# Attention, layer norm and a mixture of experts on one core: two early projections, one transfer for the row maxima, and the norm stage's tail mixed with the first shared block

## The reference

```python
q = q * cos + rotate_half(q) * sin;  k = k * cos + rotate_half(k) * sin
attn = softmax(einsum('bqhd,bkhd->bhqk', q, k) * scale);  out = einsum('bhqk,bkhd->bqhd', attn, v)
x = layernorm(x + out @ Wo)
normed = x * rsqrt(mean(x ** 2) + 1e-08) * norm_weight
shared = relu(normed @ sw1 + sb1) @ sw2 + sb2
probs = sigmoid(normed @ router_w.T);  scores, idx = top_k(probs, 2)
w = scores / (sum(scores) + 1e-06)
routed = sum over the two chosen e of w_e * (relu(normed @ ew1[e] + eb1[e]) @ ew2[e] + eb2[e])
x = layernorm(x + shared + routed)
```

## Time and profile before

| | |
|---|---|
| median of 3 runs | 1240.48 us (1239.56 to 1247.5) |
| the profiled execution's own time | 1242.63 us |
| its span in the trace | 1240.8 us |
| mean granted TensorE clock | 0.975 of full speed |
| busy: PE, PEld, DVE, ACT, POOL | 1168.7, 860.3, 940.9, 897.4, 580.9 us |

### The profile page before, as it was taken

How to read it: one execution, slowest core, us unless ns; L and a number is a source line. 1 busy time by engine, 2 the same in 40 slices (tenths; PEclk the granted TensorE clock), 3 DMA queues, 4 the chain that set the end, 5 groups by cost and what they waited for, 6 DMA issues and landing times. The chain is left out here.

```text
span 1240.8 us, 25922 instructions
## 1 busy us (share of the span) xinstructions
PE 1168.7 (94%) x8416; PEld 860.3 (69%) x8416; DVE 940.9 (76%) x1865; ACT 897.4 (72%) x1979; POOL 580.9 (47%) x593
## 2 busy tenths in 40 slices
PE   4799999999999999899999799999999999999897
PEld 3233333333333332278999799999999999999897
DVE  5788888888888888288666568777777777777596
ACT  5388878887788776667545367777777777777686
POOL 6232323232232200046567646666666666666763
PEclk9699999999999999999899989999999999999999
DMA  6854645565554620151132277767777777776363
GB/s 150 150 111 101 150 112 138 113 144 119 125 117 106 133 70 19 35 179 35 57 112 92 93 223 257 256 232 230 260 248 235 236 258 244 233 243 208 131 207 110
DMA packets 260826, 194.50 MB, mean 157 GB/s; under 512 B 152272, under 2 KB 243664, under 8 KB 260752
## 3 DMA queue, kind: packets, MB, share of 16 engines
q1 hardware_dynamic: 253936, 174.82, 49.8%
q0 software_dynamic: 6816, 18.75, 4.2%
HBM read 122.06 MB, written 37.52 MB: 129 GB/s over the span
## 5 line engine op out<-in xcount | busy, mean ns | idle before, releaser
L561 DVE TENSOR_REDUCE att_mx<-att_psA 128x1 f32<-128x512 f32 x512 | 328.0, 680 | 83.8 <-PE att_psA L359 83.5
L469 ACT ACTIVATE att_prob<-att_psB 128x512 f32<-128x512 f32 x512 | 293.6, 606 | 102.7 <-PE att_psB L371 100.9
L359 PE MATMUL att_psA<-att_qk 96*128 96x512 bf16 x512 | 199.0, 392 | 16.3 <-DMA att_qk<-att_prob 8.7
L371 PE MATMUL att_psB<-att_qk 128*128 128x512 bf16 x512 | 195.5, 385 | 7.7 <-DMA att_qk<-att_mrow 6.8
L1650 ACT ACTIVATE exp_psU<-exp_psU,ew_b 128x256 f32<-128x256 f32 x312 | 126.7, 447 | 103.6 <-PE exp_psU L1607 103.6
L1701 DVE CAST exp_hh<-exp_psU 128x512 fp32r<-128x512 f32 x156 | 107.8, 691 | 102.1 <-ACT exp_psU L1650 102.1
L1590 PE MATMUL exp_psD<-exp_w2h,exp_hh 128*128 128x256 f32 x624 | 175.8, 282 | 0.0
L1605 PE MATMUL exp_psU<-exp_xh,exp_w1h 128*128 128x256 f32 x624 | 173.8, 278 | 1.4 <-DVE exp_xl L1692 1.4
L1607 PE MATMUL exp_psU<-exp_xh,exp_w1l 128*128 128x256 f32 x624 | 173.3, 278 | 0.0
L1606 PE MATMUL exp_psU<-exp_xl,exp_w1h 128*128 128x256 f32 x624 | 173.3, 278 | 0.0
L1591 PE MATMUL exp_psD<-exp_w2l,exp_hh 128*128 128x256 f32 x624 | 172.4, 276 | 0.0
(11 more groups left out here) (236 smaller groups left out, 2779.7 us busy)
## 6 DMA issues: line engine op xcount, KB each, us to landing
ew_w<-ew SPq DMA_DIRECT2D x40, 1024.0 KB, 5.6
exp_w<-ew SPq DMA_DIRECT2D x38, 1024.0 KB, 5.8
slots_x<-pre_acc SPq DMA_DIRECT2D x13, 780.0 KB, 4.4
pre_spare<-slots_x SPq DMA_DIRECT2D x39, 260.0 KB, 4.2
out_g<-rows_y SPq DMA_DIRECT2D x32, 256.0 KB, 4.0
ew_b<-eb SPq DMA_DIRECT2D x39, 128.0 KB
pre_spare<-xT SPq DMA_DIRECT2D x8, 512.0 KB, 5.1
attn_rows<-att_ob SPq DMA_DIRECT2D x8, 512.0 KB, 2.8
```

The costliest lines, as they stand in the source:

```text
L359: pe.matmul(psA[A_BANK[n % U]][:, :], r[:, 0, qt * P:(qt + 1) * P], r[:, 1, :], start=True, stop=True).then_inc(s_amm, 1)
L371: pe.matmul(psB[B_BANK[n % U]][:, :], r[:, 1, kt * P:(kt + 1) * P], r[:, 0, :], start=True, stop=True).then_inc(s_bmm, 1)
L469: act.activation(prob[:, n % PR, :], psB[B_BANK[n % U]][:, :], ACT.Exp, scale=SCALE).then_inc(s_exp, 1)
L561: dve.reduce_max(mx[:, g % 2, n % U:n % U + 1], psA[A_BANK[n % U]][:, :], AX_X).then_inc(s_max, 1)
```

## The change

Three things are changed.

- **Early projections.** The query and key projections of tiles 5 and 6 are made right behind that of tile 4, ahead of the first row blocks of scores, into the free banks psB[0] and psB[1]; their rotations go to period -2 and to the end of period -1. `score_cols(1)` waits for the second.
- **Maxima.** `place_max` moves the three pieces with one transfer (48 partitions to 3) in place of three (16 partitions to 1 each).
- **Norm tail and dispatch.** PE's and ACT's slots from 34 on move into the shared stage. From slot 36 on, four slots begin with one chunk of `up` of block 0. Ahead of slot 35, ACT makes `rows_hi` of block 0 and the sigmoid of tiles 0 to 23. DVE makes `rows_lo` of block 0 and chooses the experts of those 24 tiles ahead of the wait for the norm stage, and those of the last 8 behind it. PE counts the ranks ahead of chunk 7 of block 0 instead of behind it. The eight scans become one. POOL does `hidden_lo` for block 0 only; DVE does it for block 1, behind `place`, and `rows_lo` of block 1 also goes behind `place`. POOL's memset goes to the front.

```diff
+    LATE_ASIDE, EARLY_QK = (2, 3), (5, 6)
+    EARLY_ROPE = ((FILL, ROPE[-1]), (FILL + 1, U - 1))
...
             def place_max(g):
                 sp.wait_ge(s_mev, g + 1)
-                for k in range(PIECES):
-                    sp.dma_start(qk[96 + k:97 + k, g // HG % 2, 0, heads(g), :].rearrange("o j (t c) -> o (j t) c", c=P),
-                                 mrow[k * U:(k + 1) * U, g % 2, :]).then_inc(s_mld[g % 2], 16)
+                sp.dma_start(qk[KR:KR + PIECES, g // HG % 2, 0, heads(g), :].rearrange("o j (t c) -> o (j t) c", c=P),
+                             mrow[:, g % 2, :]).then_inc(s_mld[g % 2], 16)
...
+                if n == 1:
+                    pe.wait_ge(s_qrd, EARLY_QK[1] + 1)
...
+                        if p + QK_LEAD == FILL:
+                            for tile in EARLY_QK:
+                                project(tile, False)
...
+    AHEAD, POOLED = 2, 1
+    CHOSEN = TILES - 2 * QT
+    UP_FROM, UP_IN_TAIL, RANK_BEFORE = tail.first + 2, 4, 7
...
+            for slot in range(tail.first, tail.end):
+                if slot == UP_FROM:
+                    for s, v in (tail.turned, tail.residual, tail.split):
+                        pe.wait_ge(s, v)
+                if 0 <= slot - UP_FROM < UP_IN_TAIL:
+                    shared.up(pe, Nth(0), slot - UP_FROM, slot - UP_FROM + 1)
+                tail.tensor(pe, slot)
...
+            for slot in range(tail.first, tail.end):
+                if slot == UP_FROM - 1:
+                    act.wait_ge(*tail.transposed)
+                    shared.rows_hi(act, Nth(0))
+                    act.wait_ge(*tail.residual)
+                    probabilities(slice(0, CHOSEN))
+                tail.scalar(act, slot)
             pr.after_last(act)
+            probabilities(slice(CHOSEN, TILES))
...
+            dve.wait_ge(s_k, 32)
+            shared.rows_lo(dve, Nth(0))
+            link(choose(0, slice(0, CHOSEN)))
             pr.after_last(dve)
-            shared.rows_lo(dve, Nth(0))
-            choose()
-            shared.rows_lo(dve, Nth(1))
+            link(dve.memset(ones[:, :], 1.0))
+            choose(1, slice(CHOSEN, TILES)).then_inc(s_both, 1)
+            weigh()
             place()
-            shared.rows_lo(dve, Nth(2))
+            for n in range(POOLED, AHEAD):
+                shared.rows_lo(dve, Nth(n))
+                Nth(n).wait(dve, shared.lo_ready, shared.HC, 0)
+                for h in range(shared.HC):
+                    shared.hidden_lo(dve, Nth(n), h)
+            shared.rows_lo(dve, Nth(AHEAD))
```

267 lines of the change are left out of this document (142 added, 125 removed).

## The result

| | before | changed |
|---|---|---|
| median of 20 runs each | 1243.08 us (1238.6 to 1247.5) | 1236.99 us (1232.12 to 1241.31) |
| ratio | | 0.9946, 95% interval 0.9933 to 0.9959 |
| own time of the profiled execution | 1242.63 us | 1234.07 us |
| its span | 1240.8 us | 1232.2 us |
| start of the norm stage (PE's first turning) | 523.59 | 514.83 |

The change makes the kernel 6.7 us faster by the ratio (5.1 to 8.3 by its interval), and the two medians are 6.1 us apart. The forecast was 12.7 us; 1236.99 us lies above the range. The two profiled executions are 8.6 us apart: 8.8 us had been won when the norm stage began, and from there to the load of tile 0 the changed kernel took 703.64 - 514.83 = 188.8 us, where before it took 711.96 - 523.59 = 188.4 us. By these two executions the dispatch gave nothing.

What follows compares the result with a forecast made beforehand. The prediction saw unbroken expert matmuls, entered through scatters landing 5.8 us after the last addition, and late maxima in attention. Start 3.7, transfer 5.6 and dispatch 3.4 gave 12.7 us off 1240.48: 1227.8 us, range 1221.5 to 1234.5 (8 in 10).

Steps and rivals of the forecast that it cites:

- What bounds: Entry to the experts: scatters land 5.8 us after the last addition, capping the dispatch's gain if PE's chain stays.
- Start: Start of period 0 in attention: earlier first column block 1.4, projection moved out 2.9, slow clock -0.6; 3.7 us.
- the first column block at 50.15: Period 0: one issue at 48.43 plus 1.7 us landing brings this block at 50.15 instead of 51.63, 1.4 us.
- the projection's 2.9 us: Period 0: tile 6's projection no longer stands between first and second column blocks; 2.9 us, less 0.6 for slow clock.
- Transfer: Attention's maxima: one transfer lands 1.2 us earlier than the third of three, removing waits in 8 late periods; 5.6 us.
- The rule of the Trainium skill: Maxima transfer: by it the new one uses 3 DMA engines instead of 16; the sum could fall to 7.1 us.
- the late periods: Attention from 62 us on: 8 places where PE waits for the maxima, each at most 1.1 us, 5.6 us in all.
- Dispatch: Norm stage to experts: scatters stop being the bound, tile 0's rows load at 708.6 instead of 711.96; 3.4 us gained.
- The slip of ACT: Norm tail, slot 35: `rows_hi`, table load and sigmoid delay the scaling of tile 27 from 584.26 to about 586.65.
- The choice: Behind the last logits: short sigmoid 0.3 us plus twelve operations on 64 columns, 3.2 us to the rank instead of 9.4.
- 24 matmuls of `up` done early: Norm tail: it ends 4.3 us later, but 24 of the 48 matmuls of `up` are then already done.
- the dispatch gives nothing: Rival: a new wait replaces the scatters, `place` 3.3 us longer, for instance by POOL's `hidden_lo` beside it; 1231.2 us, chance 0.1.

Runs made afterwards that it cites:

- e_attn: Kernel before plus only attention's two edits, early projections and single transfer for the maxima; ratio to before 0.9956 (0.9942 to 0.9971).
- e_early: Kernel before plus only the early projections, three transfers for the maxima kept; ratio to before 0.9996 (0.9976 to 1.0017).
- x_noup_lo: Changed kernel with no chunk of `up` in the tail and `rows_lo` of block 1 inside `place`; ratio to before 0.9934 (0.9911 to 0.9956).
- x_lo: Changed kernel with `rows_lo` of block 1 in the middle of `place` instead of behind it; ratio to before 0.9936 (0.9917 to 0.9954).
- x_best2: Changed kernel with unbroken tail, one-part choice, `rows_lo` of block 1 ahead of `place`, block 0's `rows_hi` and `rows_lo` early; 0.9894 and 0.9901 of before.
- e_tail: Kernel before plus only the new norm tail, two-part choice and dispatch, attention as it was; ratio to before 1.0017 (0.9997 to 1.0038).
- x_noup: Changed kernel with no chunk of `up` in the tail, all seven behind it; ratio to before 0.9937 (0.9919 to 0.9954).
- l_one: Changed kernel with the copy of the maxima to `mrow` two steps later, behind row 12 instead of 10; one execution, 1270.07 us.

## Why the prediction was wrong

In short: the step that failed is the dispatch, and in it the way to block 1, where the norm stage's tail and the choice were sized too short and the second fall of the clock was left out.

**What bounds.** Right. The cap of 5.8 us on the dispatch, and that PE's own chain would be the next bound once the scatters are early, are what came: the last addition now releases the rows of tile 0.

**Start, forecast 3.7 us, measured 2.4** (the second copy to `mrow` at 62.05 instead of 64.41). What failed here is the first column block at 50.15. Its weights were loaded at 52.35, later than the 51.62 of before. This row is the changed kernel's:

```profile
52.35 0.10 PEld L374 LDWEIGHTS att_psB<-att_qk 128*128 128x128 bf16 x1 [6.23 <-DMA att_qk<-att_mrow]
```

The landing there took 2.9 us from the start of the issue (49.42) and not 1.7. e_attn issued at 48.63 and had its block at 52.36 all the same, and e_early, with three transfers, at 52.12. So with the early projections that block stands at 52.1 to 52.4 whatever the transfer. What holds it are SP's four transposes of tile 4, which go out ahead of the maxima: they landed late, and the maxima land right behind them. This is their landing from the start of the issue, in the kernel before and then in the changed one:

```profile
DMA to landing us min/median/max: 3.2/3.2/3.3
```

```profile
DMA to landing us min/median/max: 3.2/4.5/5.2
```

In e_attn the last of the four landed at 52.16 and the maxima at 52.32. In all twelve executions with the early projections one of the four took 4.4 to 5.2 us; in the five without them none took over 3.5. In each of the twelve a 16 KB packet of the queue for instructions starts between 47.0 and 49.1, and the transposes' packets become few behind it; in the five it comes at 52.8 at the earliest. So the edit seems to have drawn a load of instructions into that stretch. It is a neighbour in all twelve, and not shown as the cause. The sum had no such term. The 1.7 us of landing was itself too short for the single transfer (2.3 in a normal period). The second step, the projection's 2.9 us out of period 0, was right and hid that: the second block came at 53.18 instead of 55.02, and the eighth at 58.29 instead of 60.66, where about 57 was named.

**Transfer, forecast 5.6 us, measured 6.4** in the trace (8.8 in all less 2.4). Right in its sum. The rule of the Trainium skill that spoke against it holds in the spread and did not come true in size. The packets in the trace show the spread: beside its 48 pieces of 256 bytes the new transfer has 3 packets of 4 bytes, where an old one has 16 of them beside its 16 pieces, as 3 engines and 16 would give. Its packets take 18 ns each and lie within 0.27 us (108.40 to 108.67), about three at a time, those of an old one within 0.18 us. In all the new transfer lands 0.5 to 0.6 us later than one of the three (2.2 to 2.3 us from the start of the issue, against 1.7), and 0.16 of that is the longer issue. The size of the step per period was wrong, 0.7 us won and not 1.2. It was enough for the late periods at the end (waits of 0.39 to 0.69 us, and one of 1.15), and the slow issues in the middle did not come back. The prediction laid the late periods to slow issues; four of the eight were the last periods, in which PE comes to its block sooner. Over all runs the two edits of attention are worth 5.5 us (3.6 to 7.2), not the 8.8 of the trace.

**Dispatch, forecast 3.4 us, measured -0.4** (from the two traces; the ratios put it at 1.2 us won on top of attention's edits and 2.1 lost without them). This is the step that failed. Against the forecast, all from the start of the norm stage:

| | forecast | measured |
|---|---|---|
| scaling of tile 27 | 63.1 | 63.5 |
| last logits copied (end) | 71.9 | 74.1 |
| rank | 75.2 | 79.8 |
| `slot` (end) | 82.9 | 87.8 |
| block 1 | 85.9 | 89.8 |
| last addition done | 185.0 | 188.8 |

The slip of ACT was right, and that the clock falls; that it stays at half through the first three chunks, 6 us and more, was sized too low, and with it the tail by 2.2 us. The choice was sized at 3.2 us and took 5.2, because POOL worked beside it, and from the logits to the rank it was 5.7 us instead of 3.3; the prediction named that very mechanism in a rival, for `place`, and gave it 0.1. The price of the second fall of the clock, behind PE's wait for the rank, was not in the sum at all. And the prediction took 24 matmuls of `up` done early as a gain that stands against the late tail; x_noup_lo against x_lo, one execution of each, has block 1 2.5 us later with them than without. The rival "the dispatch gives nothing" is what happened.

**Sum and base.** The forecast is missed by 1236.99 - 1227.8 = 9.2 us. Of these, 4.1 lie in the spans (1232.2 instead of 1228.1): 3.8 in the dispatch, 0.5 in attention, the rest the other way. The other 5.1 lie between a span and a median: the median of 3 runs, 1240.48, was 2.6 us below that of 20, and the profiled execution of the changed kernel is 2.9 us below its own median, where that of the kernel before is 0.5 below. With 9 us between the fastest and the slowest run of one kernel, a range of 13 us around a median of three was too narrow by itself. Counted as a gain, the range began at 1240.48 - 1234.5 = 6.0 us, and the medians of 20 are 6.1 us apart: with a better base the number would have come in at the edge, by luck, with the dispatch still wrong. Two small slips: the upper bound by its own terms (start 3.7, dispatch 2) is 1234.8 and not 1234.5, and the slip of ACT ends at 586.61 and not 586.65.

## What to carry to other kernels

Work put into a gap is worth only what the chain behind it gets earlier: ask when the next consumer begins, not how many matmuls are done, and whether the granted clock is low in that gap. A helper engine that gets its work earlier also gets in the way earlier, here POOL beside DVE's two-input operations. Where a producer's latency is just covered, look at its late cases and not at its median: the single transfer is 0.65 us earlier as a rule, and was worth 6.4 us in the trace because the late ones went. And an edit that only moves work can move other traffic with it: here, it seems, a load of instructions came to lie beside the transposes.

## What the hardware showed that was not expected

The matmuls of the shared blocks have two paces at the same granted clock. These rows are the stretch from 630 to 690 us, first of two executions of x_best2, then of two of e_tail, the same code in each pair (us, busy PE, PEld, DVE, ACT, POOL, PEclk, DMA share, GB/s):

```profile
630.00:690.00 60.00, 60.00 (x532) 60.00 (x531) 39.21 (x87) 29.40 (x72) 45.46 (x45) 1.00 0.27 96
```

```profile
630.00:690.00 60.00, 60.00 (x512) 60.00 (x511) 37.15 (x83) 26.68 (x65) 45.03 (x46) 1.00 0.27 98
```

```profile
630.00:690.00 60.00, 60.00 (x532) 60.00 (x531) 41.16 (x92) 29.70 (x73) 45.26 (x45) 1.00 0.27 96
```

```profile
630.00:690.00 60.00, 60.00 (x512) 60.00 (x511) 38.43 (x89) 29.54 (x72) 44.90 (x47) 1.00 0.27 96
```

One matmul starts every 0.1133 us or every 0.1177 us, without a wait recorded in either. An execution keeps one of them from where the clock has come back to full, in block 0 or 1, to the last addition: 98.3 us or 102.0 (1.5 us more where the clock also fell at block 1). Of the 15 executions of the table 6 had the slow one, which moves the whole time by 3.7 us; e_tail and x_best2 each had either, so that it is not the code's. What sets it is open.

A wait of PE costs more than itself if the clock falls behind it. In e_tail PE waited 2.96 us for `rows_lo` of block 1, and in the 5 us behind it the granted clock was 0.71, with 31 matmuls recorded instead of 43 to 47; the same came behind the 2.3 us of its second execution and the 2.2 us of x_noup (0.66 and 29 matmuls in both). In the changed kernel the waits of 1.14 and 1.03 us in the same place had no such effect. l_one, which has the same code there, waited 2.3 us and had the clock at 0.66 again: the changed tail can go either way, and goes the dearer one in the three executions in which PE did not wait for the rank.

A transfer of 48 pieces of 256 bytes by SP takes 0.75 us to issue and lands 2.3 us (median) behind the start of the issue; one of 16 takes 0.59 us and lands after 1.7. Three times the pieces are 0.6 us.

Late transfers and loads of instructions lie side by side. This is the packet of e_attn between 48.4 and 49.6 us, in which its transposes slow down (packets, MB, share of 16 engines):

```profile
q8 instruction: 1, 0.02, 4.9%
```
